# A first and an eighth step in another order, and three expert down weights loaded early

## The chip, the cores and the metric

The kernel runs on one core of one Trainium2 chip. The metric is device time in microseconds, as the median of several executions of the same program.

## What is computed

One post-norm transformer layer over 16 sequences of 256 tokens with 256 channels, all in float32. A retention-style attention (8 heads, rotary shift, decay mask, no softmax) with a gated group norm is followed by a layer norm. A mixture of 8 experts with top-1 routing plus a shared expert, both of hidden width 512, is followed by a second layer norm. Cut to its core:

```python
q, k, v, g = x@w_q+b_q, x@w_k+b_k, x@w_v+b_v, x@w_g+b_g
sim = einsum(shift(q), shift(k)/scale) * gamma**(n-m)   # causal
ret = group_norm(sim @ v) * gn_weight + gn_bias          # per head
x1  = layernorm(x + (silu(g)*ret) @ w_o + b_o)
logits = x1 @ router_w.T; e = argmax(logits); s = sigmoid(max(logits))
routed = (up_e(s*x1) * silu(gate_e(s*x1))) @ down_e
shared = (silu(x1@sh_gate) * (x1@sh_up)) @ sh_down
out = layernorm(x1 + shared + routed)
```

## The kernel before, in words

The work is written out by hand, one program for each engine, held together by semaphores. Sequences go in pairs of 512 tokens (four tiles of 128), numbered 0 to 7. The steps of the main loop run over t = 0 to 9; in the text the first step is t = 0, the eighth is t = 8 (`PAIRS`) counted by its index. Step t projects queries, keys, values and gate of pair t, runs the attention of pair a = t - 1, and the router and the shared expert of pair f = t - 2. Most products use a high and a low part of both operands, so three matmuls for each (`three`); the products of the last two shared pairs and the experts' down use plain float32.

PSUM is four pairs of banks, `duo[0]` to `duo[3]`. `x1_duo(f)` names the pair that takes the transposed x1 and the router's results of pair f.

At the start SyncE loads x, the small biases, the 1 MB rotation table `rot` and two more biases; ScalarE's queue loads the weights of queries, keys, gate and values in this order. ScalarE makes the high part of each weight and VectorE the low one. VectorE also centres the value weights over each head (`center`). `products` multiplies a projection with the rotation table, `swap` shuffles, and GpSimd adds both into `turned`, which the similarities need. GpSimd also makes the low part of pair 1's x (`second_x_lo`), which lies in x1T's memory.

In the routing, `choose` finds the best expert of each token from the logits, `rank` is a pair of small matmuls that counts the tokens ahead of each, `find_seats` turns this into a seat number, and GpSimd scatters token numbers and scores into the table `seat_d` (`take_seats`: some small operations and four indirect DMAs). `plan_early` fixes which expert each of the first 21 slots of 128 seats serves.

After the steps come 39 slots. SyncE loads the seats of a slot (`seat_load`), GpSimd gathers their rows of x1 and shared sum (`gather`), the TensorE transposes them (`slot_transposes`, the first one inside the last `shared_down`), runs gate and up of the slot's expert, transposes the product and multiplies with the down weights; GpSimd scatters the normalised rows out. Expert weights lie in memory that earlier tensors of the steps give up: `w_gu` is loaded in steps 3 to 8, the down weights `w_dn` 4 and 7 in step 9, 5 and 6 after the first seat loads, and 0 to 3 by ScalarE's queue when the last shared gate-up is done. `expert_lo` and `expert_rest` subtract the high from the whole weights on VectorE and GpSimd.

In step 8 VectorE does the group norm, then `choose`, then the gate product; GpSimd does the last layer norm's scales (`norm_scales(7)`) before `take_seats(6)`; and two weight subtractions follow the last shared product.

Of the kernel before, what the change touches and what calls it, by code (L numbers as in the profile page):

```python
# [24 lines left out]
F32R = mybir.dt.float32r  # L25
# [20 lines left out]
ROWS = 5  # L46
OUTS = 4
# [9 lines left out]
def build(nc, x, w_q, b_q, w_k, b_k, w_v, b_v, w_g, b_g, w_o, b_o, gn_w, gn_b, router_w,  # L57
          gate_up, down, sh_gate, sh_up, sh_down, x_t, rotation, squares, token_seats, free_seats, out):
    ctx = ExitStack()
    with ctx:  # L60
# [75 lines left out]
        seat = sb("seat", [P, SLOTS, SEAT], I32)  # L136


        places = ExitStack()
        with places:  # L140
# [4 lines left out]
            x1T = p_sb("x1T", [P, 2, KT, TOK], F32R)  # L145
            x1 = p_sb("x1", [P, TILES, D])
# [105 lines left out]
        class sig:  # L252
# [3 lines left out]
            bias_in = new("bias_in")  # L256
            c_in = new("c_in")
# [8 lines left out]
            center = new("center")  # L266

# [160 lines left out]
        def _(sp):  # L428

            sp.dma_start(x_in[:, :, :], x_t[0].rearrange("p (k n) -> p k n", k=KT)).then_inc(sig.xin, 16)  # L430
            sp.dma_start(bias_qk[:, 0, :], b_q.rearrange("(p two) -> p two", two=2)).then_inc(sig.first_in, 16)
            sp.dma_start(bias_qk[:, 1, :], b_k.rearrange("(p two) -> p two", two=2)).then_inc(sig.first_in, 16)
            sp.dma_start(rot[:, :, :], rotation.rearrange("p (f n) -> p f n", f=8)).then_inc(sig.first_in, 16)
            sp.dma_start(bias_v[:, :], spread(b_v)).then_inc(sig.bias_in, 16)
            sp.dma_start(bias_g[:, :], b_g.rearrange("(p k) -> p k", k=KT)).then_inc(sig.bias_in, 16)
            sp.wait_ge(sig.xT_lo, KT)
            sp.dma_start(x_in[:, :, :], x_t[1].rearrange("p (k n) -> p k n", k=KT)).then_inc(sig.xin, 16)
            sp.wait_ge(sig.first_in, 16 * 3)
            sp.wait_ge(sig.wv_in, 16)
# [28 lines left out]
            def step(t):  # L468
# [54 lines left out]
            sp.wait_ge(sig.gu_ps, 2 * FT * PAIRS)  # L523
            down_in(5)
            down_in(6)
# [13 lines left out]
        def _(act):  # L539
# [23 lines left out]
            for g in range(2):  # L563
                cols = slice(P * g, P * (g + 1))
                nc.scalar.activation(wqk[:, :, 0, :, cols], raw_qk[:, :, :, cols], ACT.Copy).then_inc(sig.w_hi, 1)
            act.wait_ge(sig.wg_in, 16)
            nc.scalar.activation(wvg[:, 0, :, D:2 * D], raw_vg[:, :, D:2 * D], ACT.Copy).then_inc(sig.w_hi, 1)
            act.wait_ge(sig.center, 5)
# [1333 lines left out]
```

## Time and profile before

| | |
|---|---|
| median of 3 executions | 595.92 us (594.05 to 597.69) |
| profiled execution, its own time | 595.46 us |
| its span, first to last instruction | 593.7 us |
| TensorE busy | 556.3 us, 94% of the span |
| VectorE, GpSimd, ScalarE busy | 391.9, 301.2, 225.5 us |
| mean granted TensorE clock | 0.986 of full speed |

Busy is time in which an engine has an instruction running; a busy TensorE need not be at its peak. The span is shorter than the time, which also holds what comes before the first and after the last instruction. In the rows PE is the TensorE, PEld its weight load, DVE VectorE, ACT ScalarE, POOL GpSimd, SPq SyncE's queue; L1581 is a line of the kernel. Matmuls in plain float32 show as two records each.

### The profile page before, as it was taken

Reading aid. Unit: us, or ns where it says so; the run is one execution under the profiler, and the core shown is the slowest. Engines: PE = TensorE matmul, PEld = TensorE weight load, DVE = VectorE, ACT = ScalarE, POOL = GpSimd, SP = SyncE. Lnnn points to the kernel's source line nnn. Section 1 sums busy time; section 2 is a strip of 40 time slices with the busy share of each in tenths; the row PEclk is TensorE's granted clock in tenths of the full one; section 3 lists DMA queues with packets and bytes.
Section 4 is the critical chain, followed back from the end, with each engine's and each line's share of the span. In section 5 each row is a group of like instructions: output and inputs, shape, how many; then the busy total and the mean of one; then the engine's idle time right before and its main releaser. Section 6 shows DMA issues by size and latency. Waiting matters only on the chain.

```text
span 593.7 us, 11148 instructions
## 1 busy us (share of the span) xinstructions
PE 556.3 (94%) x3718; PEld 457.9 (77%) x3718; DVE 391.9 (66%) x825; ACT 225.5 (38%) x403; POOL 301.2 (51%) x312
## 2 busy tenths in 40 slices
PE   5898989999999999999997998899999999999990
PEld 4677778887797897897895876688888888888870
DVE  4888987888877878778676777156654444444441
ACT  2434532552542543433436751233333333333320
POOL 1444592481571661761841576156665555555532
PEclk9999999999999999999999999799999999999996
DMA  7801206202203203200753245622343222222200
GB/s 258 288 3 37 72 2 72 72 1 72 72 2 72 72 2 72 72 23 19 261 196 110 106 112 161 207 55 80 61 94 83 80 73 72 80 81 81 80 28 18
DMA packets 36998, 50.48 MB, mean 85 GB/s; under 512 B 10528, under 2 KB 29472, under 8 KB 36800
## 3 DMA queue, kind: packets, MB, share of 16 engines
q1 hardware_dynamic: 27696, 31.24, 18.0%
q0 software_dynamic: 6048, 15.39, 9.0%
q10 hardware_dynamic: 3200, 3.15, 1.7%
q8 instruction: 32, 0.52, 0.4%
q14 instruction: 22, 0.18, 0.1%
HBM read 36.21 MB, written 13.96 MB: 85 GB/s over the span
## 4 chain that ended last, share of the span: by engine, by line
PE 74%; issue 11%; POOL 7%; DVE 4%; DMA 2%; ACT 0%; POOLq 0%; SPq 0%; DVEq 0%
PE duo L1451 41%; PE duo L1800 11%; PE duo L1655 5%; PE duo L1505 4%; PE duo L1527 3%; PE duo L1810 3%; PE duo L1659 2%; POOL turned L801 2%; POOL rstd L818 2%; PE duo L1645 1%; DMA rot<-rotation 1%; POOL x_res L824 1%; PE duo L1593 1%; PE duo L1581 1%; PE duo L1566 1%
## 5 line engine op out<-in xcount | busy, mean ns | idle before, releaser
L1451 PE MATMUL duo<-w_gu_hi,xsT 128*128 x312 | 107.1, 404 | 0.0
L1451 PE MATMUL duo<-x1T,wsgu 128*128 128x512 f32 x384 | 93.4, 395 | 0.0
L1451 PEld LDWEIGHTS duo<-x1T,wsgu 128*128 128x128 f32 x384 | 70.9, 188 | 15.2
L1401 DVE SCALAR_TENSOR_TENSOR eh<-duo,seat,e_act 128x512 f32<-128x512 f32 x39 | 29.3, 751 | 77.0 <-PE duo L1451 68.7
L1800 PE MATMUL duo<-w_dn,ehT 128*128 x312 | 73.8, 379 | 0.8 <-ACT ehT L783 0.8
L801 POOL TENSOR_TENSOR turned<-turned,swapped 128x1024 f32<-128x1024 f32 x16 | 38.1, 2399 | 69.0 <-DVE swapped L980 69.0
L1451 PEld LDWEIGHTS duo<-w_gu_hi,xsT 128*128 128x128 f32 x312 | 59.1, 189 | 11.2
L920 POOL DMA_INDIRECT out_rows<-of,seat x39 | 39.7, 1017 | 55.2 <-DVE of L1420 52.8
L1800 PEld LDWEIGHTS duo<-w_dn,ehT 128*128 128x128 f32 x312 | 56.2, 190 | 7.1 <-issue 1.0
L1451 PE MATMUL duo<-w_gu,xsT 128*128 x156 | 61.1, 392 | 0.0
L576 ACT ACTIVATE sims<-duo 128x256 f32<-128x256 f32 x64 | 21.1, 381 | 82.8 <-PE duo L1505 82.5
L989 DVE TENSOR_TENSOR sims<-duo,causal 128x512 f32<-128x512 f32 x64 | 41.2, 686 | 16.2 <-ACT sims L576 15.9
L911 POOL DMA_INDIRECT xz<-xz_d,seat x39 | 43.5, 1116 | 14.1 <-DMA seat<-seat_d 6.5
L783 ACT ACTIVATE ehT<-duo 128x512 f32<-128x512 f32 x39 | 23.4, 599 | 69.7 <-PE duo L1810 44.7
L818 POOL TENSOR_TENSOR rstd<-var_e,minus_half 128x16 f32<-128x16 f32 x16 | 46.9, 2945 | 0.7
L830 POOL TENSOR_SCALAR ln_e<-mv 128x4 f32<-128x4 f32 x8 | 1.8, 228 | 82.1 <-DVE mv L1088 82.1
L776 ACT ACTIVATE e_act<-duo,seat 128x512 f32<-128x512 f32 x39 | 26.9, 690 | 35.0 <-PE duo L1451 35.0
L868 POOL DMA_INDIRECT seat_d<-stage,place_i x32 | 33.5, 1047 | 13.2 <-issue 8.3
L1451 PE MATMUL duo<-xT,wqk 128*128 128x512 f32 x144 | 39.0, 409 | 0.0
L1505 PEld LDWEIGHTS duo<-turned 32*128 32x128 f32 x512 | 26.2, 184 | 14.8 <-issue 10.7
L1505 PE MATMUL duo<-turned 32*128 32x128 f32 (+1 forms) x512 | 34.1, 349 | 3.5 <-issue 2.0
L1655 PE MATMUL duo<-wsd_s,hT_hi 128*128 128x256 f32 x192 | 35.2, 285 | 1.8 <-DVE hT_lo L1055 1.8
(169 smaller groups left out, 1131.5 us busy)
## 6 DMA issues: line engine op xcount, KB each, us to landing
w_gu<-L_ffn_gate_up_proj SPq DMA_DIRECT2D x8, 1024.0 KB, 7.0
x_in<-x_t SPq DMA_DIRECT2D x8, 512.0 KB, 6.1
x_res<-L_attn_x SPq DMA_DIRECT2D x8, 512.0 KB, 4.0
xz_d<-zs SPq DMA_DIRECT2D x8, 512.0 KB, 4.8
xz_d<-x SPq DMA_DIRECT2D x7, 512.0 KB, 4.9
w_dn<-L_ffn_down_proj SPq DMA_DIRECT2D x4, 512.0 KB
w_dn<-L_ffn_down_proj ACTq DMA_DIRECT2D x4, 512.0 KB
rot<-rotation SPq DMA_DIRECT2D x1, 1024.0 KB, 8.6
```

The source lines that it names most:

```text
L776: nc.scalar.activation(e_act[:, :], duo[s % 2][:, 0, :], ACT.Silu, scale=f32(seat[:, s, :])[:, 2:3])\
L801: nc.gpsimd.tensor_tensor(turned[:, g, :, :], turned[:, g, :, :], swapped[:, g, :, :], ALU.add)\
L818: nc.gpsimd.tensor_tensor(rstd[:, half], var_e[:, half], minus_half[:, half], ALU.pow)\
L868: pool.indirect_dma_start(seat_d, bass.IndirectOffsetOnAxis(ap=place_i[:, q:q + 1], axis=0), stage[:, q, :], None).then_inc(sig.scat, 16)
L911: pool.indirect_dma_start(xz[:, s % ROWS, :], None, known, bass.IndirectOffsetOnAxis(ap=seat[:, s, 0:1], axis=0))\
L920: pool.indirect_dma_start(out, bass.IndirectOffsetOnAxis(ap=seat[:, s, 1:2], axis=0), of[:, s % OUTS, :], None).then_inc(sig.out_done, 16)
L989: nc.vector.tensor_tensor(sims[:, j % 4, :, 0::2, :], src, mask, ALU.mult).then_inc(sig.s_diag, 1)
L1401: nc.vector.scalar_tensor_tensor(out=eh[:, :], in0=duo[s % 2][:, 1, :], scalar=f32(seat[:, s, :])[:, 2:3], in1=e_act[:, :], op0=ALU.mult, ...
L1451: last = mm(out_, left(a, k), right(b, k), start=start and k == 0 and n == 0, stop=stop and k == kt - 1 and n == len(PASSES) - 1)
L1505: last = mm(sim_duo(a, j)[:, i % 2, SEQ * kb:SEQ * kb + SEQ - P * kb], turned[rows, g, 1, key:key + P], turned[rows, g, 0, key:SEQ * (b + 1)],
L1655: last = mm(duo[2][:, q // 2, D * (q % 2):D * (q % 2 + 1)], left[:, q * P:(q + 1) * P], wsd_s[:, b, n, :], start=n + m == 0, stop=n == FT ...
L1800: last = mm(duo[2][:, 1, 0:D], ehT[:, f, :], dn_flat[:, bass.ds(e * (FT * D) + f * D, D)], start=(f == 0), stop=(f == FT - 1))
```

## The change

The first step. Seven matmuls on a zeroed tile (`BLANKS`) run before the first projection. The rotation table is loaded in four parts with a semaphore each, the first one directly behind x; ScalarE's queue loads the value weights before those of the gate. VectorE centres the value weights first and makes their low part before that of the gate; V is projected before the gate, whose banks are now `duo[3]` in this step. The later weights' high parts move to behind the second off-diagonal copy.

The memory. `x1T` and `x1` get a home of their own, outside the memory that `w_dn` takes over, and a blank of 3 x 1024 elements stands in their old place. The ring for GpSimd's DMA descriptors shrinks from its default of 16384 to 4096 bytes a partition, which frees the same 12 KB. The down weights of experts 5, 6 and 7 are loaded in step 6, and nothing is loaded for them later.

The eighth step. x1 of pair 6 is transposed into `duo[0]`. x1's transposes signal for each half; those of the last pair go tile by tile, as each tile of x1 is ready. VectorE does half of the group norm, `choose`, the other half, a shared product, `find_seats` and then the gate product; output sums and their statistics go by halves; `plan_early` moves to before the first of the two weight subtractions, which waits for the norm's scales, and the second moves behind the shared sums. `rank` moves to before the y transposes. GpSimd takes the seats before the last norm's scales. `choose` is cut in two, its last copy is `go_on`. The split of the shared down into two halves, with the last x1 transposes and the first slot's transposes in between, is in both kernels.

```diff
+BLANKS = 7
+        x1T = sb("x1T", [P, 2, KT, TOK], F32R)
+        x1 = sb("x1", [P, TILES, D])
-            x1T = p_sb("x1T", [P, 2, KT, TOK], F32R)
-            x1 = p_sb("x1", [P, TILES, D])
+            early_dn = p_sb("early_dn", [P, 3 * FT * D])
...
+            if t == 0:
+                return duo[3][:, k, :]
             return duo[2][:, 1, :] if t == 1 else duo[1][:, k, :]
+        def x1T_duo(f):
+
+            return duo[0] if f == PAIRS - 2 else x1_duo(f)
...
+            sp.dma_start(rot[:, 0:2, :], rotation.rearrange("p (f n) -> p f n", f=8)[:, 0:2, :]).then_inc(sig.rot_in[0], 16)
...
-            sp.dma_start(rot[:, :, :], rotation.rearrange("p (f n) -> p f n", f=8)).then_inc(sig.first_in, 16)
...
+            rot_part(1)
             sp.dma_start(bias_v[:, :], spread(b_v)).then_inc(sig.bias_in, 16)
+            rot_part(2)
+            rot_part(3)
...
+                if t == PAIRS - 2:
+                    down_in(5)
+                    down_in(6)
+                    down_in(7)
...
-                    sp.wait_ge(sig.x1_out, 16 * PAIRS)
-                    down_in(7)
...
-            sp.wait_ge(sig.gu_ps, 2 * FT * PAIRS)
-            down_in(5)
-            down_in(6)
...
+            act.dma_start(raw_vg[:, :, 0:D], k_rows(w_v)).then_inc(sig.wv_in, 16)
             act.dma_start(raw_vg[:, :, D:2 * D], k_rows(w_g)).then_inc(sig.wg_in, 16)
-            act.dma_start(raw_vg[:, :, 0:D], k_rows(w_v)).then_inc(sig.wv_in, 16)
...
+                        if t == 1 and j == 1:
+                            later_weights_hi()
...
+                if has(f) and t <= PAIRS:
+                    take_seats(f)
                 if t == PAIRS:
                     norm_scales(a)
-                if has(f) and t <= PAIRS:
-                    take_seats(f)
...
+            products(0, 1)
+            rest_of_vg(3, slice(0, D))
...
             swap(0, 0)
+            rest_of_vg(4, slice(D, 2 * D))
             products(0, 2)
+            dve.wait_ge(sig.center, 5)
+            v_biased(0)
             products(0, 3)
-            v_biased(0)
             swap(0, 1)
...
+                        group_norm(a, [0])
+                        choose(f)
+                        group_norm(a, [1])
                         shared_product(f, 1)
-                        choose(f)
+                        go_on(f)
+                        find_seats(f)
                         gated(a)
...
                     if t == PAIRS:
+                        plan_early()
+
+                        dve.wait_ge(sig.nmr_ok, PAIRS)
                         expert_lo(1, 3)
-                        expert_lo(2, 4)
...
                     if t == PAIRS:
-                        plan_early()
+                        expert_lo(2, 4)
...
+                if f == PAIRS - 1:
                     for q in range(TILES):
-                        last = nc.tensor.transpose(x1_duo(f)[:, k, q * P:(q + 1) * P],
-                                                   x1_of(f)[:, q, k * P:(k + 1) * P], ident[:, :])
-                last.then_inc(sig.x1T_ps, 1)
+                        pe.wait_ge(sig.x1_ok, TILES * f + q + 1)
+                        for k in range(KT):
+                            last = turn_tile(k, q)
+                            if q == TILES - 1:
+                                last.then_inc(sig.x1T_ps, 1)
...
+            pe.wait_ge(sig.blank_ok, 1)
+            blank = y[:, 0:2, :].rearrange("p q d -> p (q d)")
+            for n in range(BLANKS):
+                mm(duo[0][:, 0, 0:D], blank[:, 0:P], blank[:, 0:D], start=True, stop=True)
             for s in range(4):
                 project(0, s)
+            v_project(0)
             gate_project(0)
-            v_project(0)
...
                     if t == PAIRS:
+                        rank(f)
                         y_transposes(a)
...
-    nc = bacc.Bacc("TRN2", target_bir_lowering=False, num_devices=1)
+    nc = bacc.Bacc("TRN2", target_bir_lowering=False, num_devices=1, dynamic_dma_scratch_size=4096)
```

## Rows read from the trace of the kernel before

**Rows 1.** Windows, TensorE: stretch, length, busy us (instructions), granted clock, DMA share, GB/s.

```profile
104.00:276.60 172.60, 172.60 (x1381) 1.00 0.17 47
387.00:577.00 190.00, 190.00 (x967) 1.00 0.27 73
...
374.00:376.00 2.00, 2.00 (x7) 0.50 1.03 353
```

**Rows 2.** Chain that ended last: start us, length us, what ran.

```profile
369.10 4.28 issue
373.38 0.66 PE duo L1645 x2
374.04 3.41 PE duo L1659 x8
377.45 3.48 PE duo L1451 x12
...
387.57 2.74 PE duo L1451 x12
...
392.70 2.74 PE duo L1451 x12
...
579.98 2.49 DMA out_rows<-of,seat
```

**Rows 3.** Timeline, 343 to 365: start, length, engine, line, operation, count, [idle before].

```profile
343.49 4.48 DVE L1093 TENSOR_TENSOR w_gu<-w_gu,w_gu_hi 128x2048 fp32r<-128x2048 f32 x2
...
344.61 1.22 POOL L839 TENSOR_TENSOR nmr<-nm,ln_r 128x4 f32<-128x4 f32 x1
...
355.17 0.96 POOL L868 DMA_INDIRECT seat_d<-stage,place_i  x1 [0.30 <-issue]
356.15 4.62 POOL L844 TENSOR_TENSOR w_gu<-w_gu,w_gu_hi 128x2048 fp32r<-128x2048 f32 x1
...
362.08 5.21 SPq L516 DMA_DIRECT2D seat<-seat_d  x5
...
364.57 2.89 POOL L911 DMA_INDIRECT xz<-xz_d,seat  x1 [3.79 <-DMA seat<-seat_d]
```

**Rows 4.** Timeline of TensorE in the eighth and ninth steps.

```profile
321.52 1.06 PE L1581 MATMUL duo<-ident,x 128*128 128x128 f32 x8 [0.81 <-ACT retT L583]
...
324.60 1.10 PE L1593 MATMUL duo<-x1T,wr 128*16 128x512 f32 x4 [1.14 <-DVE x1T L1002]
...
332.96 1.04 PE L1635 MATMUL duo<-ident,y 128*128 128x128 f32 x8
...
347.99 1.09 PE L1581 MATMUL duo<-ident,x_last 128*128 128x128 f32 x8 [1.18 <-ACT x_last L656]
...
351.10 1.09 PE L1593 MATMUL duo<-x1T,wr 128*16 128x512 f32 x4
```

**Rows 5.** Timeline of the start, four engines; the first matmul row is cut at 10.1.

```profile
7.04 3.32 PE L1467 MATMUL duo<-xT,wqk 128*128 128x512 f32 x7 [7.04 <-ACT wqk L565]
...
7.04 7.19 PE L1467 MATMUL duo<-xT,wqk 128*128 128x512 f32 x24 [7.04 <-ACT wqk L565]
...
10.60 0.63 ACT L567 ACTIVATE wvg<-raw_vg 128x512 fp32r<-128x512 f32 x1 [3.19 <-DMA raw_vg<-L_attn_w_g]
...
12.65 0.68 DVE L1272 TENSOR_REDUCE mean_v<-raw_vg 128x16 f32<-128x512 f32 x1
...
16.02 0.68 DVE L1260 TENSOR_TENSOR wvg<-raw_vg,wvg 128x512 fp32r<-128x512 f32 x1
...
18.06 2.40 POOL L801 TENSOR_TENSOR turned<-turned,swapped 128x1024 f32<-128x1024 f32 x1 [15.65 <-DVE swapped L980]
...
21.87 0.94 PE L1505 MATMUL duo<-turned 32*128 32x256 f32 x16 [1.97 <-issue]
...
22.98 1.66 PE L1451 MATMUL duo<-x1T,wqk 128*128 128x512 f32 x6 [0.18 <-POOL x1T L807]
```

**Rows 6.** One line's instructions: count, duration ns min/median/max, first and last start.

```profile
L839 POOL TENSOR_TENSOR nmr<-nm,ln_r x8: 198/199/1217, 62.9 to 344.6; 128x4 f32<-128x4 f32 x8
```

More of the change, by code:

```diff
@@ L256, in build @@
             bias_in = new("bias_in")
+            bias_g_in = new("bias_g_in")
             c_in = new("c_in")
@@ L266, in build @@
             center = new("center")
+            blank_ok = new("blank_ok")
+            rot_in = [new(f"rot_in{i}") for i in range(4)]
             xin = new("xin")
@@ L600, in x1_hi @@
                         act.wait_ge(sig.qk_ps, 4 * 2)
-                    nc.scalar.activation(x1T[:, 0, k, :], x1_duo(f)[:, k, :], ACT.Copy).then_inc(sig.x1T_hi, 1)
+                    nc.scalar.activation(x1T[:, 0, k, :], x1T_duo(f)[:, k, :], ACT.Copy).then_inc(sig.x1T_hi, 1)
             def gate_act(t, parts=range(KT)):
                 for k in parts:
-                    act.wait_ge(sig.bias_in, 16 * 2)
+                    act.wait_ge(sig.bias_g_in, 16)
                     act.wait_ge(sig.g_ps, KT * t + k + 1)
@@ L1012, in variance, with group_norm @@
                         .then_inc(sig.var_ok, 1)
-            def group_norm(a):
+            def group_norm(a, halves=range(2)):
                 if a == 0:
                     dve.wait_ge(sig.zrow_out, 16)
-                for i in range(2):
+                for i in halves:
                     dve.wait_ge(sig.rstd_ok, 2 * a + i + 1)
@@ L1340, in _ @@
                         choose(f)
+                        go_on(f)
                         h_low(f, 0)
                         shared_product(f, 1)
-                    group_norm(a)
-                    h_low(f, 1)
-                    if t == PAIRS:
+                        group_norm(a)
+                        h_low(f, 1)
+                        shared_product(f, 2)
+                        find_seats(f)
+                        h_low(f, 2)
+                    else:
+                        group_norm(a, [0])
+                        choose(f)
+                        group_norm(a, [1])
                         shared_product(f, 1)
-                        choose(f)
+                        go_on(f)
+                        find_seats(f)
                         gated(a)
-                    shared_product(f, 2)
-                    find_seats(f)
-                    h_low(f, 2)
-                    if t == PAIRS:
-                        output_sum(a)
-                        statistics(a)
+                        shared_product(f, 2)
+                        for i in range(2):
+                            output_sum(a, [i])
+                            statistics(a, [2 * i, 2 * i + 1])
                         moments(a)
@@ L1480, in project @@
                     pe.wait_ge(sig.z_ok, at(2 * (t - 2) + s + 1))
+                    if t == 1:
+                        pe.wait_ge(sig.gate_ok, s + 1)
                 else:
@@ L1578, in x1_transposes, with turn_tile @@
                         pe.wait_ge(sig.prod_ok, 4 * 2 + 2)
-                for k in range(KT):
+                def turn_tile(k, q):
+                    return nc.tensor.transpose(x1T_duo(f)[:, k, q * P:(q + 1) * P],
+                                               x1_of(f)[:, q, k * P:(k + 1) * P], ident[:, :])
+                if f == PAIRS - 1:
                     for q in range(TILES):
-                        last = nc.tensor.transpose(x1_duo(f)[:, k, q * P:(q + 1) * P],
-                                                   x1_of(f)[:, q, k * P:(k + 1) * P], ident[:, :])
-                last.then_inc(sig.x1T_ps, 1)
+                        pe.wait_ge(sig.x1_ok, TILES * f + q + 1)
[3 more added lines that the diff above has]
+                                last.then_inc(sig.x1T_ps, 1)
+                else:
+                    for k in range(KT):
+                        for q in range(TILES):
+                            last = turn_tile(k, q)
+                        last.then_inc(sig.x1T_ps, 1)
             def router(f):
```

52 lines of the change are left out of this document (30 added, 22 removed).

## The prediction

> **What bounds the kernel now.** I read the windows first. From 104 to 276.6 us, steps three to six, the TensorE is busy for 172.6 of 172.6 us, and in the expert slots, from 387 to 577 us, for 190 of 190, both at clock 1.00 [rows 1]. The change adds and removes no arithmetic there, so neither stretch can give or cost time unless another engine becomes the limit. What can move lies in three places where the TensorE waits: the start, the eighth step with the head of the ninth, and the hand-over to the slots.
>
> The chain of waits shows the hand-over [rows 2]. The TensorE stands still for 4.28 us from 369.10, until the rows of slot 0 are gathered. What follows is slow: the last eight matmul records of the shared down take 3.41 us and the first gate-up 3.48, where later slots take 2.74. The windows give the reason: after this rest the granted clock is 0.50 from 374 to 376, so 1.2 GHz instead of 2.4 [rows 1].
>
> Why is the gather late? SyncE issues the first seat load only at 362.08 [rows 3]. The code has it wait for the four seat scatters of the seventh pair, the last of which GpSimd issues at 355.17, because they stand in its queue behind the last norm's scales [rows 3]. Then GpSimd takes 2.89 us over the first gather, at 364.57 [rows 3], and its data shares the DMA engines with six loads of down weights; from 374 to 376 they move 353 GB/s [rows 1]. The TensorE can go on at 373.38, 8.8 us after the gather's start.
>
> In the eighth step the TensorE waits 0.81 us for a copy out of PSUM (x1 transposes), 1.14 for x1T before the router and 1.18 for the last x1 [rows 4]. At the start it waits for 7.04 us for the first weights, runs its first seven matmuls in 3.32 us where all 24 take 7.19, and waits 1.97 us before the first similarities [rows 5].
>
> **The start.** The seven blank matmuls run before 7.04, while the TensorE is idle anyway. From the rows, seven matmuls take some 3.1 us start to start while the other 17 take 3.9: 0.44 against 0.23 us each, the ratio of the two clock levels. If the blanks raise the clock, the first product ends at about 12.5 instead of 14.2. The Trainium skill, TensorE: Matmul & The Clock Gate, part 1 (The HAM clock gate), says that idleness is the throttled default and activity releases it; by that the blanks work, and the row agrees in what real matmuls did. That the blanks are zeros I can't judge from the trace, so I keep both cases. It matters little, because V's weights bind next. They now have the third place on ACT's queue, whose load was there at 10.60 [rows 5]. From that, VectorE sums and centres them, makes the second product and the low part. Before, this took from 12.65 to 16.70, 4.05 us; one bias operation of about 0.35 is moved behind it. So V can start between 14.3 and 14.65; I take 14.45. V and gate ran from about 14.05 to 19.90 before, 5.85 us without a gap; now they end at 20.3. The first similarities start at 20.4 instead of 21.87. Meanwhile the shuffle and GpSimd's 2.40 us addition [rows 5] give the turned queries at about 18.5, and VectorE reaches V's bias by 19.5, both hidden under gate. The next projection needs x1T's low half, which GpSimd has 2.5 us after the addition (20.46 to 22.98 before): 21.1, so it starts at 21.45 instead of 22.98. Only moving the weight copies between the second and third off-diagonal copy costs anything: ScalarE's 2.75 us there delay one mask by 0.9 us of a lead of 1.5, and the next group catches up. **Term: -1.4 us**, bounds -0.4 (V's weights a microsecond later) and -1.6.
>
> **The eighth step.** The x1 transposes go to a free PSUM pair, so they no longer wait for the copy: 0.75 us. The copy back can begin after four of eight transposes, another 0.4: the router starts at 323.45, not 324.60. Half is lost again. The ranks now stand before the y transposes and need the chosen experts, which VectorE has at about 331.8 (first half of the group norm at 329.6, 0.65 us, then 1.6 of small steps); the second half of the norm follows, so the y transposes start at 332.75 instead of 332.96, and the output 0.3 earlier. The 1.18 us before the last x1 transposes is what goes away for good. Its cause is in GpSimd's queue and VectorE's: the last scale took 1.22 us [rows 3], while its median is 0.20 [rows 6], because two weight subtractions of 2.24 us each began at 343.49 [rows 3]. After, the subtraction waits for that scale. The Trainium skill, SBUF — State Buffer, section Who interferes with whom, has the rule: a VectorE instruction with two SBUF inputs and a GpSimd one that reads SBUF exclude each other. The row agrees, and the rule also speaks against the change, since the moved seat scores now lie beside the gate product; by it they could be 1.3 us later, of which the queue has slack for about one. Seat scores and scatters run from 333.5 to 342.2, then the scales to 344.0, x1 to 346.1, so the transposes follow the shared down at 346.45 instead of 347.99. The early plan (2.6 us) and one subtraction (2.24) now stand ahead of the shared sum on VectorE; they end at 347.65, and x1T is done at 349.6. Router 7 starts at 349.65 instead of 351.10. **Term: -1.45 us**, bounds 0 and -2.2.
>
> **The hand-over.** Scatters end at 342.2 and land at most 7 us after the last is issued (355.17 to 362.08 before), before SyncE asks. SyncE's loads of experts 5, 6 and 7 are gone from here, so five seat loads start at 350.7. GpSimd still does its weight subtraction first, 4.62 us [rows 3]; it needs ScalarE's copy, ready at 353.2, so it ends at 357.9 and the gather starts at 358.2 instead of 364.57. Even with the 8.8 us of before it is there at 367.0. The TensorE asks at 369.10 - 1.45 = 367.65. So the 4.28 us go, and with them the low clock: 3.41 becomes 1.70, the transposes 0.66 become 0.35, the gate-up 3.48 becomes 2.74, together 2.75. **Term: -7.0 us**. Margin 0.65 us in the worst sum; some 4 with a gather free of loads. The expert weights' subtractions on VectorE end at 367.3, slot 0 wants them at 369.75. The four down loads left on ACT's queue, 2 MB from 362.2, are in by about 370 at 350 GB/s [rows 1]; slot 0's down starts at 377.
>
> **The rest.** The three early loads, 1.5 MB, are issued in step seven (t = 6) on a SyncE queue that next waits for a sum; they delay nothing. The two homes cost memory only, bought from the descriptor ring. The trace doesn't show what the ring's size does; nearest are the indirect transfers, about 1 us of GpSimd each, two in a slot of 5.13 us (387.57 to 392.70 [rows 2]). I take 0.
>
> Sum: -1.4 - 1.45 - 7.0 = -9.85. The profiled execution took 595.46 us (span 593.7), 0.46 below the median of 595.92. So 585.6 against its own execution, 586.1 against the median; I say **585.8**. Its own range is 584.4 to 587.5.
>
> **Rivals.**
> - *The slot head waits for something else* (gather, last subtraction, down weights): 1 to 4 us of the 7 stay, with some low clock; 587.5 to 591. For: three queues were retimed together. Against: margins of 0.65 to 4 us. 0.17.
> - *The start gives nothing*, because the weights land later among the reordered loads or the blanks delay the first projection: 587.2. 0.10, within the likeliest range.
> - *The eighth step gives nothing or more*: GpSimd's queue, with scatters ahead of the scales, sets x1. Each microsecond past 1 costs one; 587 to 589. 0.10.
> - *The small ring holds GpSimd.* If a transfer had to wait for the earlier one to land, which takes the last one 2.49 us [rows 2], a slot would need about 1.0 + 2.5 twice and 0.8 of scales, 7.8 us; GpSimd decides from 5.13 us a slot on. 39 x 2.7 = 105 us: about 690, slower. Partly so, 600 to 640. For: the ring is a quarter. The Trainium skill, DMA: Bandwidth & Descriptors, The descriptor swizzle, counts nine descriptors per engine for a 128-partition transfer, and each of 16 bytes (Terms); by it 4096 bytes hold 28 transfers, and the rival falls. 0.05.
> - *The retimed order gains further*, at the slots' head: 582 to 584.4. 0.06.
> - The likeliest as summed: 0.52.
>
> A measurement here tells about 0.5% (3 us) from no change. Faster by more (below 592.9) is 0.92, within 0.03, slower 0.05. The 8-in-10 range takes the likeliest with the start and step cases and most of the first rival: 583.2 to 589.8.
>
> **What would show it.** No TensorE gap near 368 and a granted clock of 1.00 through the hand-over; seat loads at about 351; the gather at about 358; similarities at 20.4; router 7 at 349.65; slots still 5.13 us. Wrong if the gap stays, if slots lengthen, or if a new wait stands at the y transposes or before slot 0's down.

## The result and the profile after

The changed kernel takes 578.7 us (median of 4 runs, 578.61 to 578.91), the kernel before 594.98 (592.62 to 597.69): a ratio of 0.971, with a 95% interval of 0.968 to 0.974. It is faster, as I said, but by 16.3 us where I had forecast 9.85, and below my range of 583.2 to 589.8.

The page of the changed kernel, parts 1 and 2 (the granted clock in 40 slices):

```profile
span 576.8 us, 11184 instructions
...
PE 558.0 (97%) x3732; PEld 458.9 (80%) x3732; DVE 391.8 (68%) x826; ACT 225.6 (39%) x403; POOL 302.8 (52%) x311
...
PEclk9999999999999999999999999999999999999998
```

**At the hand-over** stands what I forecast. The chain of waits after, which answers to [rows 2] (its longest pieces):

```profile
365.99 1.73 PE duo L1710 x8
367.71 2.77 PE duo L1484 x12
370.50 0.76 DVE eh L1433
371.97 2.79 PE duo L1484 x12
374.98 1.73 PE duo L1856 x8
377.14 2.76 PE duo L1484 x12
```

No wait of TensorE precedes slot 0: the whole chain has slot 0's transposes at 365.77, directly behind the shared down. The last eight records of the shared down take 1.73 us instead of 3.41 and the gate-up 2.77 instead of 3.48. The windows give the clock of this stretch (columns: stretch, length, then PE, PEld, DVE, ACT and POOL, clock, DMA share, GB/s):

```profile
368.00:374.00 6.00, 5.38 (x27) 4.27 (x26) 1.52 (x3) 2.26 (x4) 0.00 (x0) 1.00 0.86 283
```

The reason is in the timeline after, against [rows 3]:

```profile
350.59 4.81 SPq L537 DMA_DIRECT2D seat<-seat_d  x5
...
356.48 2.90 POOL L929 DMA_INDIRECT xz<-xz_d,seat  x1 [0.17 <-issue]
...
360.62 2.97 ACTq L780 DMA_DIRECT2D w_dn<-L_ffn_down_proj  x4
```

Seat loads at 350.59 (I said 350.7), the gather at 356.48 (I said 358.2, from 364.57), now 4 us ahead of ScalarE's four loads of down weights. Slots stay at 5.14 us (377.14 to 382.28).

**In the steps**, TensorE's timeline, against [rows 4]:

```profile
322.03 1.09 PE L1644 MATMUL duo<-x1T,wr 128*16 128x512 f32 x4 [0.70 <-DVE x1T L1022]
...
330.75 1.07 PE L1686 MATMUL duo<-ident,y 128*128 128x128 f32 x8
...
344.65 1.04 PE L1620 MATMUL duo<-ident,x_last 128*128 128x128 f32 x8
...
348.00 1.10 PE L1644 MATMUL duo<-x1T,wr 128*16 128x512 f32 x4 [0.15 <-DVE x1T L1022]
```

**At the start**, the timeline of TensorE, against [rows 5]:

```profile
1.46 5.40 PE L1763 MATMUL duo<-y 128*128 128x256 f32 x14 [1.46 <-DVE y L1273]
7.84 5.72 PE L1500 MATMUL duo<-xT,wqk 128*128 128x512 f32 x24 [0.99 <-ACT wqk L583]
14.66 3.14 PE L1484 MATMUL duo<-wvg,xT 128*128 128x256 f32 x24 [1.10 <-DVE wvg L1284]
17.64 2.91 PE L1484 MATMUL duo<-xT,wvg 128*128 128x512 f32 x12
20.48 0.94 PE L1540 MATMUL duo<-turned 32*128 32x256 f32 x16
21.59 1.67 PE L1484 MATMUL duo<-x1T,wqk 128*128 128x512 f32 x6 [0.18 <-POOL x1T L825]
```

**The rest is at the very end.** The last slot's down starts at 568.34 instead of 578.25, 9.91 us earlier: that is my sum of 9.85. But the span is 16.9 us shorter. The ends of the two chains, before first, then after:

```profile
582.51 0.50 issue
583.01 1.28 POOLq L60
```

```profile
570.08 2.52 DMA out_rows<-of,seat
572.60 0.03 issue
572.64 0.50 issue
573.14 1.30 POOLq L61
```

The last row of each is GpSimd's queue at the line that closes the program. From its start to the end of the span it is 10.7 us before (583.01 to 593.7) and 3.7 after. The trace's record there is GpSimd's closing DRAIN: 10.43 us before, 3.45 after. 9.91 + 6.98 = 16.89. TensorE is long done then and no engine computes; the last scatter is still under way at first, but in both kernels its last packet ends 2.4 us after the drain's start.

### The profile page after: what moved, and what is told of

The parts are those of the page before. It is cut to its first block, busy times and chain, and to the rows that moved or that the text cites. A ratio compares the mean times of both kernels' runs of the same rounds, so it can differ in the third digit from the quotient of the medians.

```text
span 576.8 us, 11184 instructions
## 1 busy us (share of the span) xinstructions
PE 558.0 (97%) x3732; PEld 458.9 (80%) x3732; DVE 391.8 (68%) x826; ACT 225.6 (39%) x403; POOL 302.8 (52%) x311
## 4 chain that ended last, share of the span: by engine, by line
PE 84%; DVE 5%; issue 4%; POOL 3%; ACT 1%; DMA 0%; POOLq 0%; DVEq 0%; ACTq 0%
PE duo L1484 47%; PE duo L1856 11%; PE duo L1706 6%; PE duo L1540 5%; PE duo L1562 4%; PE duo L1866 3%; PE duo L1696 1%; PE duo L1750 1%; PE duo L1710 1%; PE duo L1644 1%; POOL turned L819 1%; PE duo L1686 1%; PE duo L1602 1%; PE duo L1620 1%; DVE sims L1009 1%
## 5 line engine op out<-in xcount | busy, mean ns | idle before, releaser
L929 POOL DMA_INDIRECT xz<-xz_d,seat x39 | 45.2, 1158 | 8.9 <-issue 4.9
L886 POOL DMA_INDIRECT seat_d<-stage,place_i x32 | 36.1, 1130 | 13.2 <-issue 7.5
```

The source lines that it names most:

```text
L886: pool.indirect_dma_start(seat_d, bass.IndirectOffsetOnAxis(ap=place_i[:, q:q + 1], axis=0), stage[:, q, :], None).then_inc(sig.scat, 16)
L929: pool.indirect_dma_start(xz[:, s % ROWS, :], None, known, bass.IndirectOffsetOnAxis(ap=seat[:, s, 0:1], axis=0))\
```

## The experiments

Times are medians; the kernel before, run beside each of them, took 595.4 to 595.8 us. Where nothing else is said, a diff is against the kernel before.

### The ring alone

```diff
-nc = bacc.Bacc("TRN2", target_bir_lowering=False, num_devices=1)
+nc = bacc.Bacc("TRN2", target_bir_lowering=False, num_devices=1, dynamic_dma_scratch_size=4096)
```

> The kernel before with only the descriptor ring cut from 16384 to 4096 bytes a partition. Theory: the closing drain on GpSimd, 10.43 us before and 3.45 after, follows the ring's size; then the drain is about 3.5 us here and the time falls by 7.0, to about 588 by the median (span about 587), with everything up to the last transfer as before. Rival 1: the drain is shorter because of the new order of transfers; then it stays near 10.4 and the time doesn't move. Rival 2, from the prediction: the small ring holds GpSimd; then slots take more than 5.13 us.

588.39 us (587.6 to 589.13), ratio 0.988 [0.987, 0.990]. Its chain:

```profile
369.10 3.97 issue
...
582.58 1.28 POOLq L60
```

The gap before slot 0 is still there (3.97 us), the first similarities still start at 21.87 and router 7 at 351.10; the drain takes 3.44 us. With 8192 in place of 4096:

> The kernel before with a ring of 8192 bytes. If the drain is linear in the ring's size, the two known points (16384: 10.43, 4096: 3.45) give 0.582 us per 1024 bytes and 1.12 fixed, so 5.8 us here and a time 4.65 us below before. If the drain falls only from some size on, it is 10.4 or 3.5.

591.16 us (590.47 to 592.1), ratio 0.993 [0.991, 0.995], drain 5.86 us. That is what the line through the two sizes gave (5.8). And 2048, in the changed kernel:

> The changed kernel with a descriptor ring of 2048 bytes in place of 4096. The closing drain took 10.43, 5.86 and 3.44 us with rings of 16384, 8192 and 4096 bytes. Theory: about 0.58 us for each 1024 bytes and about 1.1 us besides, so 2.3 us here: 578.7 less 1.2, 577.3 to 577.8 us, all else unchanged. Rival: the gathers of a slot no longer fit into the ring at once, GpSimd waits for room in it, and rows reach the slots late: idle time of TensorE in the slots, 580 us or far more. The trace tells them apart by GpSimd's times for the gathers and by the spacing of the slots, 5.13 us in both kernels.

578.28 us (577.81 to 578.37), ratio 0.971 [0.969, 0.973], drain 3.37 us. The line through three sizes broke here: 0.08 us less, not 1.1. So something else sets a floor, and the size was not the whole cause. The slots keep their spacing, but GpSimd is held, mostly for some 0.3 us and once for longer: the fifteenth indirect DMA starts 5.54 us behind the fourteenth, where the changed kernel has 1.79. TensorE is busy throughout (30.00 of the 30 us from 200 to 230).

```profile
214.72 1.49 POOL L886 DMA_INDIRECT seat_d<-stage,place_i  x1 [0.30 <-issue]
220.26 0.96 POOL L886 DMA_INDIRECT seat_d<-stage,place_i  x1 [4.05 <-issue]
```

### What the drain goes by

Small kernels that only copy x to the output, and leave out the whole layer, stand in for the full one; each ran once, under the profiler. The first two have the ring of 16384 bytes. This is GpSimd's part in the first, where SyncE copies the other 28 tiles; in the second GpSimd has no part, and SyncE copies all:

```diff
+for t in range(4):
+    pool.indirect_dma_start(out, bass.IndirectOffsetOnAxis(ap=rows[:, t, 0:1], axis=0),
+                            held[:, t, :], None).then_inc(seats_done, 16)
+pool.wait_ge(seats_done, 64)
```

> Not this kernel's work: 28 tiles of x are copied to the output by one transfer of SyncE, 4 by indirect DMAs of GpSimd, and all are waited for; the ring has the size that the kernel before has (16384 bytes). Theory: the closing drain of GpSimd costs about 10.4 less what the last landing takes, 9 to 10.5 us, however few descriptors have passed through the ring, since it goes by the ring's size. Rival: it goes by the descriptors that the kernel has put there, and after 4 indirect DMAs in place of over 100 it takes under 3 us.

> Not this kernel's work: all 32 tiles of x are copied to the output by one transfer of SyncE; GpSimd does nothing, and the ring has the size that the kernel before has (16384 bytes). Theory: the drain looks at the ring whether or not GpSimd issued anything, 9 to 10.5 us. Rival: without an indirect DMA in the kernel there is nothing to drain, under 1 us, and the price is one of kernels with indirect DMAs alone.

The drain took 0.39 us with four indirect DMAs. Without any, GpSimd's drain came at once and took 0.04. My theory of the size alone fell, so the next runs changed the count. Each has `for k in range(N)` with a wait after every DMA; t16k_4_last leaves out the last wait; t16k and t4k stand for rings of 16384 and 4096 bytes.

> Not this kernel's work: 32 tiles of x go to the output by 32 indirect DMAs of GpSimd, each waited for, with the ring of 16384 bytes. The closing drain took 0.39 us after 4 indirect DMAs and 10.43 us after the 110 of the kernel before. Theory A (the drain goes by the descriptors that have passed through the ring, until it is full): between them, 2.5 to 10.5 us, more than the 0.39. Theory B (it goes by the transfer that is still under way, and by the ring's size only then): 0.4 us, as nothing is under way. Theory C (every indirect DMA adds about 0.1 us, without an end): 3.1 us.

> Not this kernel's work: the 32 indirect DMAs four times over, 128 in all, each waited for, ring of 16384 bytes. Theory A: the ring is full, 9.5 to 10.5 us as in the kernel before with its 110. Theory B: 0.4 us, nothing is under way. Theory C: 128 by 0.1 us, 12.5 us.

> Not this kernel's work: the same 128 indirect DMAs, each waited for, with the ring of 4096 bytes. Theory A: a quarter of the ring, 2.3 to 3.0 us by the slope of 0.58 us for each 1024 bytes, and less than the 3.44 us of the changed kernel if that holds the end of its last scatter. Theory B: 0.4 us. Theory C: 12.5 us, the ring's size would not matter.

> Not this kernel's work: 4 indirect DMAs with the ring of 16384 bytes, and the last is still under way when the drain begins, as in the kernel before. Theory A: few descriptors, so only what the last scatter still needs to land, 1 to 3 us. Theory B: 9 to 10.5 us, as in the kernel before.

2.67, 1.29, 1.37 and 2.84 us. A, B and C all fail: A and C want more after 128 than after 32, B wants 0.4 at 32. The last is the scatter under way, some 2.4 us, and not the ring. From 0.39 at 4 and 2.67 at 32 an indirect DMA costs 0.081 us of the drain; by that 128 leave 15 with the large ring (128 - 15 = 113) and 16 with the small one (128 - 16 = 4 x 28). Two counts on either side of 113 were to decide:

> Not this kernel's work: 110 indirect DMAs, each waited for, ring of 16384 bytes: as many as the kernel before issues. Theory D (the drain goes by the indirect DMAs since the ring was last full, 0.081 us each and 0.07 besides, full after 113): 110 of them, 8.98 us. Rival E (the drain grows to some maximum near 32 and falls again, or has a short period, as 2.67 us at 32 and 1.29 at 128 allow too): anything from 0.4 to 4 us.

> Not this kernel's work: 118 indirect DMAs, each waited for, ring of 16384 bytes, eight more than in the run beside it. Theory D: 118 less 113 is 5, so 0.48 us (0.3 to 0.6 if the ring fills after 112 to 115): eight DMAs more make the drain 8.5 us shorter. Rival E: within 1 us of the run with 110.

9.05 us with 110, 0.47 with 118. Where the ring is full, one DMA starts late. GpSimd's timeline with 118; the count stands at 113 before the third row:

```profile
311.72 0.96 POOL L81 DMA_INDIRECT out_rows<-held,rows  x1 [1.70 <-DMA out_rows<-held,rows]
314.37 0.96 POOL L81 DMA_INDIRECT out_rows<-held,rows  x1 [1.70 <-DMA out_rows<-held,rows]
318.60 0.97 POOL L81 DMA_INDIRECT out_rows<-held,rows  x1 [3.27 <-issue]
321.27 0.96 POOL L81 DMA_INDIRECT out_rows<-held,rows  x1 [1.71 <-DMA out_rows<-held,rows]
```

4.23 us from start to start in place of 2.66. In t4k_128 the same happens after 28, 56, 84 and 112, with 3.24 us. The drain, by the indirect DMAs since the ring was last full; for the full kernels this is a count that takes 113, 56, 28 or 14 DMAs to fill it:

```
kernel          ring   indirect  since full  0.081 n + 0.07  drain us
tiny_indirect   16384      4          4           0.39          0.39
t16k_32         16384     32         32           2.66          2.67
t16k_110        16384    110        110           8.98          9.05
t16k_118        16384    118          5           0.48          0.47
t16k_128        16384    128         15           1.29          1.29
t4k_128          4096    128         16           1.37          1.37
before          16384    110        110           8.98         10.43
b_ring8k         8192    110       54 (est.)      4.44          5.86
changed          4096    110       26 (est.)      2.18          3.45
a_ring2k         2048    110       12 (est.)      1.04          3.37
```

The full kernels with 16384, 8192 and 4096 bytes add 1.3 to 1.45 us, about what the last scatter's issue takes, whose row (583.25, 1.05 us) lies inside the drain that starts at 583.01. At 2048 another 1.0 us remains. There the last scatter may set the floor: its last packet ends 2.4 us into the drain. At 4096 it may do so as well, since both give about 3.4.

So the kernel before has nearly the worst count there is: it issues 110 indirect DMAs, the ring takes 113 and never fills, and the small kernel with 110 has the same drain less those 1.4 us. For the full kernels whose ring did fill, the count is not shown. If each filling emptied the ring, the changed kernel would be late after 28, 56 and 84. The pauses that the kernel before doesn't have stand before the 57th, 73rd, 84th and 103rd, 0.4 to 0.5 us each, and only the first of them fits; these are the others:

```profile
469.83 1.01 POOL L938 DMA_INDIRECT out_rows<-of,seat  x1 [1.89 <-DVE of L1452]
...
498.21 1.08 POOL L929 DMA_INDIRECT xz<-xz_d,seat  x1 [0.70 <-issue]
...
547.04 1.01 POOL L938 DMA_INDIRECT out_rows<-of,seat  x1 [2.00 <-DVE of L1452]
```

With 8192 bytes the last pause is before the 101st. Counted from these, 8 and 10 would be left, and the drains some 2.0 and 2.3 us by the same sum (an estimate), not 3.45 and 5.86. A ring that is still nearly full at the end (28 and 56) fits as well as the count. That a smaller ring bounds the drain is shown by the run with the ring alone; how much of a full kernel's ring is free after it has filled is not. The Trainium skill, DMA: Bandwidth & Descriptors, The descriptor swizzle and Terms, counts nine descriptors of 16 bytes on each engine for a transfer of 128 partitions; by that, an estimate, a ring holds 113 and 28 transfers with 16384 and 4096 bytes, and the pauses of the small kernels agree with both. What the chip does in 0.081 us a transfer no run shows.

### The start

No blanks, in the changed kernel (`BLANKS = 0`):

> The changed kernel without the seven blank matmuls. If V's centred weights bind the start, as predicted, the colder first projection costs only what its first product comes later for VectorE: 0 to 0.7 us, so 578.7 to 579.4. If the blanks carried the start's 1.4 us, the time is 580.1 and the first similarities move from 20.4 back to about 21.8.

579.73 us (579.42 to 580.03), ratio 0.974 [0.972, 0.975]; its median is 1.03 above the changed kernel's, between the two expectations; the first similarities, at 21.77, are where the second had them. TensorE:

```profile
7.79 8.44 PE L1500 MATMUL duo<-xT,wqk 128*128 128x512 f32 x24 [7.79 <-ACT wqk L583]
16.06 3.03 PE L1484 MATMUL duo<-wvg,xT 128*128 128x256 f32 x24
...
21.77 0.94 PE L1540 MATMUL duo<-turned 32*128 32x256 f32 x16
```

The first 24 products take 8.44 us instead of 5.72 (from 9 to 11 us TensorE runs 6 of them here and 11 behind the blanks), VectorE's first product waits until 10.79 instead of 9.56, and everything behind it moves, V's low part included. And the blanks in the old order, with the ring of 4096:

```diff
+nc.vector.memset(y[:, 0:2, :], 0.0).then_inc(sig.blank_ok, 1)
...
+for n in range(7):
+    mm(duo[0][:, 0, 0:D], blank[:, 0:P], blank[:, 0:D], start=True, stop=True)
```

> The kernel before with a ring of 4096 bytes and the seven products of blanks ahead of its first projection; VectorE and GpSimd keep their old order in the start. Beside it stands the kernel before with that ring alone, 588.39 us with the first similarities at 21.87. Theory A: the clock alone gives the 1.0 to 1.4 us of the start, since VectorE's first products wait for the cold projection (1.74 us of idle time without blanks): 587.0 to 587.4 us, similarities at 20.5 to 20.9. Theory B: with the old order of VectorE and GpSimd their low parts of the gate's and of V's weights (12.65 and 18.06 us in the kernel before) bind whatever the clock: 588.0 to 588.6 us, similarities at 21.4 to 21.9, and blanks and order give something only together.

588.23 us (587.57 to 590.57), ratio 0.989 [0.986, 0.992], beside 588.39: theory B, though a little of A shows in the trace, where the similarities start at 21.46. V waits for its low part until 16.35 whatever the clock:

```profile
7.24 5.95 PE L1468 MATMUL duo<-xT,wqk 128*128 128x512 f32 x24
13.02 2.88 PE L1452 MATMUL duo<-xT,wvg 128*128 128x512 f32 x12
16.35 3.13 PE L1452 MATMUL duo<-wvg,xT 128*128 128x256 f32 x24 [0.45 <-DVE wvg L1261]
```

First similarities: 21.87 with neither, 21.77 with the order alone, 21.46 with the blanks alone, 20.48 with both. Each alone gives 0.1 to 0.4 us, both together 1.39.

### The early down weights, and the order

The changed kernel with the three loads where they were:

```diff
-if t == PAIRS - 2:
-    down_in(5); down_in(6); down_in(7)
...
+sp.wait_ge(sig.x1_out, 16 * PAIRS)
+down_in(7)
...
+sp.wait_ge(sig.gu_ps, 2 * FT * PAIRS)
+down_in(5); down_in(6)
```

> The changed kernel with the down weights of experts 5, 6 and 7 loaded where they were before (7 after the last x1 store, 5 and 6 behind the first five seat loads and the last shared gate-up). Theory of the prediction: the hand-over's gain comes mostly from the earlier seat loads, and the early weights add margin; then it stays within 1 us, 578.7 to 579.7, with at most a short wait before slot 0. Rival: without the early loads the gather lands late again beside 3 MB of weights; then the gap of 4.3 us and the low clock return and the time is 583 to 586.

582.35 us (581.35 to 584.6), ratio 0.978 [0.976, 0.979]: the loads are worth 3.65 us in the median, and neither theory named the place. The profiled execution was the slowest, 584.6, so its waits are longer than the median's. There is no gap before slot 0. The wait is at slot 0's down, whose weights take 14.66 us from issue to landing:

```profile
364.16 14.66 DMA w_dn<-L_ffn_down_proj
378.82 0.24 issue
379.06 3.16 PE duo L1857 x8
```

The eight products take 3.16 us where 1.73 is usual, at a clock below full after the rest (0.62 from 379 to 382). The other way round, the old orders with ring, homes and the early loads (the diff leaves out the ring and the homes):

```diff
+if t == PAIRS - 2:
+    down_in(5); down_in(6); down_in(7)
...
-sp.wait_ge(sig.x1_out, 16 * PAIRS)
-down_in(7)
...
-sp.wait_ge(sig.gu_ps, 2 * FT * PAIRS)
-down_in(5); down_in(6)
```

> The kernel before with a ring of 4096 bytes, x1 and x1T in homes of their own and the down weights of experts 5, 6 and 7 loaded early; no order of any engine is changed, so the seats, the seat loads and the gather stay where they were. The kernel before with the small ring alone took 588.39 us, and its gap before slot 0's first product was 3.97 us. Theory: that gap is the chain of seat loads and gather on GpSimd, which the loads do not move, so the gap stays near 4 us; what the early loads save is only what waited for the weights or for the DMA engines behind them, at most 1.5 us: 587 to 588.4 us, and the reordering of step 8 is what gives the rest of the hand-over. Rival: the three loads share the DMA engines with the seat loads and the gather of slot 0, and taken out of that stretch they shorten it by most of the 3.65 us that they are worth in the changed kernel: 584.5 to 586 us, with the gap before slot 0 under 1.5 us.

583.72 us (582.61 to 589.65), ratio 0.980 [0.978, 0.983]. Better than both theories in the median, but the profiled execution was the one of 589.65, with a gap of 4.42 us. So once more:

> The kernel before with the ring of 4096 bytes and the early down weights, once more: its profiled execution took 589.65 us, and the four others 582.61 to 584.22. That execution had a stretch at half clock ahead of 48 us, and a gap of 4.42 us before slot 0. Theory: in the others the gap is shorter than in the kernel with the ring alone (3.97 us), since slot 0's gather no longer shares the DMA engines with three loads of 512 KB: a gap of 0 to 2 us, clock 1.00 at the hand-over, 583 to 584 us. Rival: the gap stays near 4 us and only the stretch at half clock after it is gone or shorter (2.75 us), so that the early loads act through what comes behind slot 0's rows: gap 3.5 to 4.5 us at 583 to 585 us.

582.78 us (582.3 to 583.56), ratio 0.978 [0.974, 0.981]; the theory's gap holds (1.18 us), its median by 0.2 us not, and the granted clock is 1.00 from 368 to 378. The first execution had 3.24 us more of gap; TensorE also came to it 1.86 us later (granted clock 0.83 from 20 to 30 us), and ran at 0.64 from 374 to 378. Timelines of the first execution, then of the second:

```profile
365.78 4.48 DVE L1093 TENSOR_TENSOR w_gu<-w_gu,w_gu_hi 128x2048 fp32r<-128x2048 f32 x2
...
365.83 3.11 POOL L911 DMA_INDIRECT xz<-xz_d,seat  x1 [3.60 <-issue]
```

```profile
363.69 1.00 POOL L911 DMA_INDIRECT xz<-xz_d,seat  x1 [3.32 <-issue]
...
363.90 4.48 DVE L1093 TENSOR_TENSOR w_gu<-w_gu,w_gu_hi 128x2048 fp32r<-128x2048 f32 x2
```

In the first the gather was issued 0.05 us after VectorE had begun a weight subtraction, and took 3.11 us; in the second 0.21 us before one, and took 1.00. A subtraction takes 2.24 us, and 0.92 us after its end the gather's issue is done (365.78 + 2.24 + 0.92 = 368.94). The Trainium skill, SBUF — State Buffer, section SBUF: two separate sides, says that a VectorE operation with two SBUF inputs and a GpSimd operation that reads SBUF take one pair of ports in turn, and the later one waits. The gather's issue reads its seat numbers from SBUF; if it counts as such an operation, the first execution agrees; in the second VectorE is the later one and is not held (4.48 us for its two subtractions in both). The two issues differ by 2.1 of the 3.24 us between the gaps; the seat loads and the landing make up the rest. Then the orders of step 8 in the changed kernel. First only GpSimd's:

```diff
-if has(f) and t <= PAIRS:
-    take_seats(f)
 if t == PAIRS:
     norm_scales(a)
+if has(f) and t <= PAIRS:
+    take_seats(f)
```

> The changed kernel, with one thing put back: in step 8 GpSimd computes the norm's scales before it scatters the seats of the router before, as the kernel before did. The changed kernel took 578.70 us. Theory: the output projection's transposes need the scales, and they are earlier on the path of TensorE, so the order of scales and seats moves at most 1 us: either the same, or up to 1 us faster, 577.7 to 578.9 us, as the seats have some microseconds of margin before the gather. Rival: the seats' scatters are what the gather waits for in the end, and GpSimd's queue is full from there to the hand-over: 579.3 to 581 us, with an idle stretch of TensorE before slot 0 that the changed kernel does not have.

578.78 us (577.99 to 581.49), ratio 0.973 [0.969, 0.977]: the same. Then the old orders of all three engines in step 8 (VectorE: the whole norm, first shared product, choice; seats behind the second shared product; output sums and statistics whole; the two subtractions together and the early plan behind them; TensorE: the ranks back behind the y transposes):

```diff
-group_norm(a, [0])
-choose(f)
-group_norm(a, [1])
+group_norm(a)
 shared_product(f, 1)
+choose(f)
...
-plan_early()
-dve.wait_ge(sig.nmr_ok, PAIRS)
 expert_lo(1, 3)
+expert_lo(2, 4)
...
+plan_early()
```

> The changed kernel with the old orders of step 8 on VectorE, GpSimd and TensorE, and all the rest kept: blanks and new start, early down weights, ring of 4096 bytes. Theory: the early loads and the reordering each stand for part of the hand-over. The kernel before with ring and early loads took 583.72 us, and the start gives 1.4, so 582.3 us (581.7 to 583.3); router 7 stands at 348.0 plus 1.7 = 349.7, the gather of slot 0 at about 364, after the burst of the shared path's and the experts' loads has begun. Rival: the early loads alone remove the wait once the start is early too, and the reordering is worth only its 1.7 us in the step: 580.0 to 580.8 us.

584.37 us (581.31 to 585.64), ratio 0.980 [0.975, 0.984]: 5.7 us slower than the changed kernel, more than either theory said, and no longer steady. Its timeline and, last, its chain:

```profile
342.39 1.56 POOL L857 TENSOR_TENSOR nmr<-nm,ln_r 128x4 f32<-128x4 f32 x1
...
344.73 1.83 PE L1616 MATMUL duo<-ident,x_last 128*128 128x128 f32 x8
...
361.17 2.05 ACTq L780 DMA_DIRECT2D w_dn<-L_ffn_down_proj  x4
362.77 2.57 POOL L929 DMA_INDIRECT xz<-xz_d,seat  x1 [3.87 <-issue]
```

```profile
367.22 3.36 issue
```

Router 7 starts at 348.46, only 0.46 us later than in the changed kernel, and 0.23 of that stand already at the first similarities (20.71). The gather is what the orders move: 362.77 against 356.48, and slot 0's rows are late again. All traces in one table (us; the first two columns are the gather's issue, start and end; then where TensorE is free for slot 0 and where it goes on; then from the issue's end to there; last, the runs):

```
kernel           issued  ends     free    goes on  after   runs, lowest to highest
before           364.57  367.46   369.10  373.38   5.92    592.62 to 597.69
b_ring4k         365.59  367.47   369.10  373.07   5.60    587.60 to 589.13
a_old_step8      362.77  365.34   367.22  370.58   5.24    581.31 to 585.64
b_early_down     365.83  368.94   370.56  374.98   6.04    582.61 to 589.65
b_early_down_2   363.69  364.69   368.70  369.88   5.19    582.30 to 583.56
a_scales_first   360.36  361.36   365.92  365.92   -       577.99 to 581.49
changed          356.48  359.38   365.77  365.77   -       578.61 to 578.91
```

While the down weights load, rows come 5.2 to 6.0 us after the issue's end, and that end jumps by 2 us with which of gather and subtraction comes first. So an issue that ends less than some 6 us ahead of 'free' leaves a gap that differs from one execution to the next. The changed kernel's meets a subtraction too (2.90 us), but with 6.4 us to spare. With the scales first 4.6 us are left, and there is no gap in this trace; ScalarE's loads had only begun (360.70) when its issue ended.

## Why the prediction was wrong

**The ring: the step that failed.** "I take 0", and the size was worth 7.0 us: the kernel before goes from 595.51 to 588.39, its drain from 10.43 to 3.44, and the rest stays. I asked what a smaller ring could hold up while transfers run, and took the nearest rows from the slots. I never read the last 10.7 us of the span, though the chain's last row (583.01, GpSimd's queue) and the span of 593.7 show them. A stretch in which no engine computes and which still counts needs an owner before the sum is made. It was a mis-sized term and not a mechanism against me: 585.6 less 7.0 is 578.6, and the profiled execution took 578.61.

**The rival "the small ring holds GpSimd"** fell in its price. A ring that fills does hold GpSimd: 0.6 us in the small kernel with 4096 bytes (3.24 in place of 2.66), 0.4 to 0.5 us in the changed kernel, 3.7 us once with 2048. But this lies where GpSimd has time, and slots stay at 5.14 us.

**The start: right size, wrong carrier.** I forecast 20.4 and 21.45, and got 20.48 and 21.59. V started at 14.66 (I said 14.45). But I called the blanks a matter of little, "because V's weights bind next". They bind through VectorE (V waits 1.10 us for them), which makes V's low part only after its first two products, and these wait for the first projection. Without blanks V starts at 16.06. The Trainium skill, TensorE: Matmul & The Clock Gate, part 1 (The HAM clock gate), says that activity releases the throttle; by that products of zeros would count as activity, and the pace of the real ones agrees: 24 in 5.72 us against 8.44. The clock itself can't be read there, since the profile gives 1.00 from 7 to 14 us in both.

**The eighth step: right size, partly the wrong source.** Without the 1.39 us of the start, router 6 came 1.18 us earlier (I said 1.15), the y transposes 0.82 (0.21), the x1 transposes 1.95 (1.54), router 7 1.71 (1.45). I gave most of it to the orders, above all to the last scale, no longer beside the two subtractions. a_old_step8 keeps that collision (1.56 us, where the changed kernel has 0.20). Its start gave only 1.17 us, and without that router 6 is 1.17 us earlier and router 7 1.47. Of the step's edits that run keeps the free PSUM pair, the copies by halves and the tile-by-tile transposes. 0.70 us of router 6's gain is left when ScalarE has the last x1 ready (347.94 before, 346.07 there). Another 0.65 comes behind it, where the x1 transposes, now tile by tile, end 0.49 us later and not 1.14. The orders give 0.2 to 0.5 at router 7.

**The hand-over: right in path and size.** -7.0 forecast, -6.81 measured (from -3.10 at router 7 to -9.91 at the last slot). The orders count here: without them the gather is issued 6.3 us later (a_old_step8). Wrong was that I gave the early loads no price ("they delay nothing"): they are 3.65 us, and without them slot 0's down waits. I had named that place among what would make me wrong, but not asked whether the loads are what keeps it free. The two parts overlap. From 588.39, the loads alone give 4.7 and 5.6 us; all but the loads gives 6.0, of which start and step are 3.1; all of it 9.7.

**The chances.** Of the rivals none came. The likeliest case came in its numbers. That the start and the eighth step fit their terms so well is in part luck, since their causes were partly others. The range missed because a cost that the trace "doesn't show" was taken as 0 with bounds on the one side only: a gain from the ring stood in none of the cases.

**Left open.** What the closing drain does for each transfer; the last 1.0 us of it with 2048 bytes; why the changed kernel pauses at the 57th, 73rd, 84th and 103rd indirect DMA; whether five indirect DMAs more would take the 7 us off the kernel before as well (not tried, and doubtful if a filling does not empty the ring there). The changed kernel with 2048 bytes is 0.4 us faster in the median, which this measurement does not tell from none.

## What to carry to other kernels

Account for the whole span before you sum, from the first instruction to the last, and give the tail a row like any other: here 10.7 us in which no engine computed held a term of 7.0 us, as large as that of the hand-over. With indirect DMAs, count them against what the ring takes: where each was waited for, the closing drain went by those since it was last full, and in the full kernel a smaller ring cut it, though no transfer is any faster. Two edits that each give little alone can give their full sum together (blanks and order), and a gather needs microseconds of lead, not tenths: beside a busy VectorE and a burst of loads its issue alone varies by 2 us.

## What the runs showed of the hardware

- In kernels that wait for each indirect DMA, GpSimd's closing drain took 0.081 us for each one since the ring was last full, and 0.07 besides: 9.05 us after 110, 0.47 after 118, with a ring that takes 113. Without indirect DMAs it took 0.04. In the full kernel, with 110, it took 10.43, 5.86, 3.44 and 3.37 us with rings of 16384, 8192, 4096 and 2048 bytes (the last in the changed kernel).
- Where each is waited for, a full ring makes the next indirect DMA late by 1.6 us (16384 bytes, after 113) or 0.6 us (4096 bytes, every 28). With 2048 bytes, in the changed kernel, the fifteenth was 3.7 us late.
- Products of zeros ahead of the real ones quicken them: the first 24 took 5.72 us behind 5.4 us of zeros and 8.44 without.
- A load of 512 KB took 14.66 us to land where six such loads were issued within 3.2 us.
- An indirect gather issued while VectorE subtracts (two inputs in SBUF) is done 0.92 us after that instruction's end, in the five traces of the table in which they met: 1.9 to 3.1 us instead of 1.0.
